# Landmark heads, token stage and passage joined anew in a convolution block, Nystrom attention and expert kernel on Trainium2

## The reference, cut to what matters

```python
# layer 0, per sample: softmax attention with 32 features, then a residual
theta, phi, g = xf @ W_theta + b_theta, xf @ W_phi + b_phi, xf @ W_g + b_g
x = x + softmax(theta @ phi.T) @ g @ W_out + b_out
# layer 1, per sample and head (8 heads of 32): attention through 128 landmarks
q, k, v = heads(layernorm(t) @ w_qkv.T); q *= 32 ** -0.5
q_l, k_l = mean of q and of k over runs of 8 tokens          # 128 landmarks
kernel_1 = softmax(q @ k_l.T); kernel_2 = softmax(q_l @ k_l.T); kernel_3 = softmax(q_l @ k.T)
t = t + (kernel_1 @ (iterative_pinv(kernel_2, 6) @ (kernel_3 @ v))) @ w_out.T + b_out
# layer 2, all tokens: 2 of 16 experts each, gelu between two matrices
t = t + sum of gate_e * (gelu(layernorm(t) @ W1_e) @ W2_e) over a token's two experts
```

## Time and profile before

| what | value |
|---|---|
| median of 3 runs | 1031.95 us (1031.53 to 1034.44) |
| profiled execution | 1034.55 us |
| its span in the trace | 1032.8 us |
| mean granted PE clock | 0.941 of full |
| PE, DVE, ACT, POOL busy | 91%, 55%, 44%, 29% |

### The profile page before, as it was taken

The page is one execution under the profiler, slowest core; times in us unless marked ns, Lnnn a source line. Parts: engine busy times, 40 slices in busy tenths (PEclk is TensorE's granted clock), DMA queues, the critical chain, the costliest instruction groups (busy, mean ns, idle before and its releaser), DMA issues.

```text
span 1032.8 us, 21740 instructions
## 1 busy us (share of the span) xinstructions
PE 936.0 (91%) x6981; PEld 703.6 (68%) x6982; DVE 569.9 (55%) x1585; ACT 449.6 (44%) x1004; POOL 298.1 (29%) x343
## 2 busy tenths in 40 slices
PE   5999989899999899998998998834889999999997
PEld 3565766465776555676655676523779999999996
DVE  3577846486866677775777684676222222222221
ACT  1424376343349352337462337524434444444442
POOL 3150002050000133000122000201357766766664
PEclk9699999698999989999999899955999999999999
DMA  3100000300000120000110000099734444443341
GB/s 102 42 2 1 1 2 25 99 1 1 2 1 2 43 81 1 1 1 2 42 42 1 1 2 1 32 224 314 219 57 71 72 65 67 70 67 63 62 64 18
DMA packets 47847, 50.76 MB, mean 49 GB/s; under 512 B 11072, under 2 KB 41152, under 8 KB 47776
## 3 DMA queue, kind: packets, MB, share of 16 engines
q0 software_dynamic: 15168, 18.85, 11.4%
q1 hardware_dynamic: 32608, 30.99, 9.9%
HBM read 33.00 MB, written 18.78 MB: 50 GB/s over the span
## 4 chain that ended last, share of the span: by engine, by line
PE 76%; DVE 10%; issue 5%; ACT 3%; DMA 3%; POOL 1%; SPq 1%; POOLq 0%; DVEq 0%; ACTq 0%
PE PS L526 13%; PE PS L941 12%; PE PS L950 12%; PE PS L795 7%; PE PS L555 6%; PE PS L587 4%; PE PS L690 3%; PE PS L671 3%; PE PS L598 3%; PE PS L592 3%; DVE neg_max L1161 2%; PE PS L650 2%; DMA low<-rows_scratch,token_of 2%; PE PS L676 2%; PE PS L685 1%
## 5 line engine op out<-in xcount | busy, mean ns | idle before, releaser
L526 PE MATMUL PS<-ident,arena 128*128 128x128 f32 x1016 | 151.1, 298 | 32.6 <-ACT arena L1007 13.3
L526 PEld LDWEIGHTS PS<-ident,arena 128*128 128x128 f32 x1016 | 126.3, 155 | 69.9 <-issue 56.4
L387 POOL TENSOR_SCALAR aggr<-aggr 128x1 f32<-128x1 f32 x64 | 14.2, 222 | 552.9 <-DVE aggr L1264 552.9
L1161 DVE TENSOR_REDUCE neg_max<-PS 128x1 f32<-128x1024 f32 (+1 forms) x96 | 117.5, 1224 | 95.3 <-PE PS L587 41.4
L941 PEld LDWEIGHTS PS<-low 128*128 128x128 f32 x1264 | 154.8, 194 | 4.6 <-DVE low L1570 0.7
L941 PE MATMUL PS<-low 128*128 128x128 f32 x1264 | 155.7, 277 | 0.0
L950 PE MATMUL PS<-arena,low 128*128 x632 | 150.2, 381 | 4.4 <-ACT low L1104 2.9
L435 POOL DMA_INDIRECT out_dram<-low,row_of x79 | 125.4, 1587 | 89.6 <-DVE low L1587 37.6
L1020 ACT COPY arena<-PS 128x1024 f32<-128x1024 f32 x96 | 98.3, 1024 | 96.9 <-PE PS L526 96.7
L950 PEld LDWEIGHTS PS<-arena,low 128*128 128x128 f32 x632 | 113.9, 190 | 18.8 <-issue 6.5
L1104 ACT ACTIVATE low<-PS 128x512 f32<-128x512 f32 x79 | 47.2, 597 | 157.9 <-PE PS L941 128.0
(11 more groups left out here) (202 smaller groups left out, 1323.0 us busy)
## 6 DMA issues: line engine op xcount, KB each, us to landing
arena<-in_L_ffn_W_dram SPq DMA_DIRECT2D x32, 512.0 KB
arena<-in_x_dram SPq DMA_DIRECT2D x4, 1024.0 KB, 6.3
out_dram<-t SPq DMA_DIRECT2D x4, 1024.0 KB, 7.2
rows_scratch<-arena SPq DMA_DIRECT2D x4, 512.0 KB, 3.4
rows_scratch<-arena SPq DMA_DIRECT2D x8, 256.0 KB, 2.6
low<-rows_scratch,token_of POOLq DMA_INDIRECT x79
out_dram<-low,row_of POOLq DMA_INDIRECT x79
arena<-in_L_attn_w_qkv_dram SPq DMA_DIRECT2D x1, 768.0 KB, 4.8
```

Source lines behind the costliest of these rows:

```text
L526: mm = pe.transpose(PS[0:s.shape[1], dst_bank, n * P:n * P + s.shape[0]], s, ident[0:s.shape[0], 0:s.shape[0]])
L1161: dve.tensor_reduce(dst, src, AX.X, ALU.max, negate=True).then_inc(s_max, 1)
```

## The change

The work is the same, and its order in the queues of PE, DVE and ACT changes at the three joins and in the token loop.

- First head: `scores(8)`, `maxima(8)` and `exponentials(8)` go ahead of the matrix pieces on their engines, and `queries(0)` goes ahead of the two transpose pieces.
- Token stage: `scores(16)` no longer waits for `queries(2)`, and `scores(17)` follows `values(14)`, before the last two pieces, which now both use bank 1; `scores(17)` waits for the 29th piece instead of the 32nd. The last piece follows `values(15)`. `queries(2)` comes just before `head_values` (now in bank 0), `queries(3)` after `scores(18)`.
- Token loop: `turn_inverses(s)` stands before `finish` and no longer waits for `out_t`; instead `out_t` waits for the next tile's `turn_inverses`, and `inverses_turned` moves behind `out_t` on DVE.
- Passage: `turn(18)` moves behind `project_tpg(1)` and into banks 2 and 3; `scores(0)`, `scores(1)`, `turn_g` follow. `turn(22)`, `gate` and the transposes back move into the next sample's opening loop (steps s = 0, 1, 2) with their DVE and ACT parts, in banks 1 and 0 (`turn_high` waits for the last normalised rows and for the next sample's g, then does `turn(22)`). On DVE `out_t(23)` goes ahead of the rows of tile 5, and `phi_out`, the last rows and `maxima(0)` are interleaved. After the last sample the router part runs as before.

```diff
+        PIECE_BANK.update({n_pieces - 1: 1, n_pieces: 1})
-                     16: 4, 17: 5, 18: 6, 19: 7, 20: 4, 21: 5, 22: 4, 23: 5}
+        UNIT_BANK.update({18: 2, 19: 3, 22: 1, 23: 0})
+        TURNS = [16, 17, 20, 21, 18, 19, 22, 23]
...
                 if k == 0 and u == 2 * NT + 1:
-                    pe.wait_ge(pinv_ev, (i + 1) * n_pieces)
+                    pe.wait_ge(pinv_ev, (i + 1) * n_pieces - 3)
...
                     if t == 0:
                         pe.wait_ge(pr_used, i * UNITS + 2 * NT)
-                    else:
-                        pe.wait_ge(ot_ready, i * UNITS + 2 * NT + t)
...
+                if i >= 1:
+                    phi_in(i)
+                    for k in range(2):
+                        scores(0, k)
                 for k in range(2):
                     scores(1, k)
-                pe.wait_ge(g_ready, i + 1)
+                if i >= 1:
+                    turn_g(i)
+                    bulk_done(19, i - 1)
                 for s in range(NT + 2):
...
+                    if s == 0 and i >= 1:
+                        turn_high(i - 1)
+                    if s == 1:
+                        pe.wait_ge(g_ready, i + 1)
+                        if i >= 1:
+                            bulk_done(23, i - 1)
+                    if s == 2 and i >= 1:
+                        gate_turned(i - 1)
                     if 1 <= s <= NT:
                         values(s - 1)
+                    if s == 1 and i >= 1:
+                        gate(i - 1)
+                    if s == 2 and i >= 1:
+                        pe.wait_ge(sample_done, i)
                     if s >= 2:
                         finish(s - 2)
...
                 pe.wait_ge(lm_ready, i + 1)
+                for k in range(2):
+                    scores(NT, k)
...
-                for k in range(2):
-                    scores(NT, k)
...
                     if s == NT - 1:
-                        pe.wait_ge(pinv_ev, (i + 1) * n_pieces - 2)
-                        queries(2)
                         pe.wait_ge(q_ready, i * 4 + 2)
...
+                    if s == NT - 1:
+                        for k in range(2):
+                            scores(2 * NT + 1, k)
+                    if s == NT:
+                        inverse_piece(*pieces[-1])
+                    if s == 0:
+                        queries(0)
-                    for piece in mine[0:2]:
+                    for piece in mine[0:2] if s < NT - 1 else mine[0:1]:
                         inverse_piece(*piece)
-                    if s < 2:
-                        queries(s)
+                    if s == 1:
+                        queries(1)
...
                 finish(2 * NT - 1)
-                for k in range(2):
-                    scores(2 * NT + 1, k)
-                pe.wait_ge(q_ready, i * 4 + 4)
+                queries(2)
                 head_values(range(HEADS)).then_inc(y_head_mm, 1)
...
+                    if s < NT:
+                        turn_inverses(s)
                     if s >= 2:
                         finish(2 * NT + s - 2)
-                    if s < NT:
-                        turn_inverses(s)
...
@@ DVE, out_t of a token tile @@
                         dve.wait_ge(inv_copied, i * NT + u - 2 * NT + 1)
+                        if u + 1 < UNITS:
+                            dve.wait_ge(inv_mm, i * NT + u - 2 * NT + 2)
...
@@ DVE, opening loop of the next sample @@
+                    if s == 0 and i >= 1:
+                        bulk(22, xT[:, 0, 512:1024], j=i - 1)
+                    if s == 2 and i >= 1:
+                        logits_out(i - 1)
                     if 1 <= s <= NT:
                         out_t(s - 1)
+                    if s == 1 and i >= 1:
+                        gate_out(i - 1)
...
@@ DVE, token loop @@
+                    if s == NT:
+                        if more:
+                            bulk(20, x0T[:, 0, 512:1024])
+                        out_t(2 * NT + s - 1)
                     if s >= 3:
                         rows1(s - 3)
...
@@ DVE, after the token loop @@
+                if more:
+                    phi_out(i + 1, 0)
+                rows1(NT - 1)
+                if more:
+                    phi_out(i + 1, 1)
+                norm1(NT - 2)
+                if more:
+                    bulk(18, xT[:, 0, 0:512])
+                    maxima(0, i + 1)
                 norm1(NT - 1)
```

More of the change, by code:

```diff
@@ L863, in _ @@
                         turn(16, xs, 0)
-                    if s == NT - 1:
-                        pe.wait_ge(xn2_ready, i * NT + NT // 2)
-                        turn(18, xn, 0)
-                        if more:
-                            turn(20, xs, 1)
+                    if s == NT - 1 and more:
+                        turn(20, xs, 1)
                     if s == NT and more:
@@ L873, in _ @@
                         project_tpg(1)
-                def gate():
-                    for c in range(KC):
-                        for j in range(QUADS):
-                            mm = pe.matmul(PS[HD * j:HD * j + HD, 3, 0:D], wgate_sb[:, c, :], xT[:, c, j * D:(j + 1) * D],
-                                           start=c == 0, stop=c == KC - 1, tile_position=(0, HD * j))
-                    mm.then_inc(gate_mm, 1)
-                pe.wait_ge(xn2_ready, (i + 1) * NT)
-                turn(22, xn, 1)
-                if more:
-                    turn_g(i + 1)
-                bulk_done(23)
-                gate()
-                if more:
-                    phi_in(i + 1)
-                    for k in range(2):
-                        scores(0, k)
-                pe.wait_ge(gate_ready, i + 1)
-                apart(pe, "pe")
-                transposes(pe, 1, [gateT[:, b * P:(b + 1) * P] for b in range(2)]).then_inc(gate_mm, 1)
+                        turn_low(i)
+                    if s == NT and not more:
+                        turn_low(i)
+            turn_high(B - 1)
+            gate(B - 1)
+            gate_turned(B - 1)
             pe.wait_ge(routed, (B + 1) * ROUTE)
@@ L1402, in _ @@
                         out_t(NT + s - 1)
+                    if s == NT - 1:
+                        maxima(2 * NT + 1)
+                        mine = mine[0:1]
+                    if s == NT:
+                        inverse_piece(*pieces[-1])
                     for piece in mine:
@@ L1419, in _ @@
                         counted(i)
-                maxima(2 * NT + 1)
-                for s in range(NT + 3):
-                    if 1 <= s <= NT:
-                        inverses_turned(s - 1)
+                more = i + 1 < B
+                for s in range(NT + 2):
                     if 1 <= s < NT:
```

129 lines of the change are left out of this document (80 added, 49 removed).

## The result

| | before | changed |
|---|---|---|
| median | 1032.69 us (1031.53 to 1034.44, 4 runs) | 1001.87 us (998.46 to 1004.54, 4 runs) |
| profiled execution, its span | 1034.55, 1032.8 us | 999.48, 997.3 us |
| mean granted PE clock | 0.941 | 0.956 |

The ratio is 0.9708, with a 95% interval of 0.9665 to 0.9752: the change makes the kernel about 31 us faster. Forecast were 1008 us, within 999 to 1024. The profiled pair differs by 35.07 us where the sum had 26.6. Executions more than 1.5% above the fastest of the same kernel enter no ratio in what follows; only the token loop alone has such, two of its four.

What follows compares the result with a forecast made beforehand. PE was taken as the bound, busy 91% of the span, with idle gaps and low-clock stretches to win: 12.1 us idle plus 9.3 and 5.2 of clock make 26.6, from 1034.55 to 1008 us, range 999 to 1024.

Steps and rivals of the forecast that it cites:

- 12.1 us of idle time: PE idle time gained over the whole kernel: 5.2 first heads, 3.2 token stage, 1.8 token loop, 1.9 passages.
- 14.5 of clock: Low-clock time won back: all 9.3 us at the first landmark heads and 5.2, half of 10.5, in the passages.
- first head: Gap of 2.41 before turn_probs(8) goes, a new one of 1.1 comes at the norm piece: 1.3 us a sample, 5.2 in all.
- token stage: Where token tiles begin, gaps of 1.4, 0.6 and 0.6 sum to 2.6 against 3.39: 0.8 us a sample, 3.2 in all.
- token loop: turn_inverses loses its wait for out_t, 0.11 us a tile in four tiles of each sample: 1.8 us in all, bounds 0 to 1.8.
- passage: Between samples, gaps of 0.9, 1.05 and 0.9 sum to 2.9 against 3.54: 0.6 us a passage, 1.9 in all.
- the rival in which the clock stays up everywhere: No low-clock stretches at heads or passages: 1034.55 - 12.1 - 19.8 = 1003 us; chance 0.20.
- the router part at its end: End of the last sample: turn(18) moves behind finish(22), but PE's wait there ends as before: 0, within 1 us either way.

Runs made afterwards that it cites:

- the token loop alone: Kernel before with only the token loop's edits (turn_inverses ahead of finish, its wait given to out_t, inverses_turned behind out_t): 998.42, 1000.48, 1015.18 and 1026.42 us.
- the run with the order put back: Changed kernel with finish again ahead of turn_inverses on PE in the token loop, waits as changed: median 1011.13 us, ratio 0.9828 to before.
- the filled kernels: Unread matmuls put in PE waits: kernel before 1009.08 us (0.9814), changed kernel 990.23 (0.963), all edits with ScalarE's bulk(19) copy later 977.97 (0.9508).

## Why the prediction was right, and where it was not

The sum was 12.1 us of idle time and 14.5 of clock. The spans of the profiled pair differ by 35.5 (1032.8 - 997.3). Of these the clock gave 9.6 at the first heads (33.96, 34.11 and 34.12 in samples 1 to 3, less 30.86 each) and 10.5 - 6.4 = 4.1 in the passages, 13.7 in all. The rest, 21.8, is what has to answer to 12.1.

| step | forecast a sample | measured a sample | by |
|---|---|---|---|
| first head | 1.3 | 1.26 | 156.58 - 155.32 |
| token stage | 0.8 | -0.13 | what is left of 156.58 - 152.37 |
| token loop | 0.45 | 3.08 | 156.58 - 153.50 |
| passage | 0.6 | 0.96 | 152.37 - 151.41 |
| sum | 3.15 | 5.17 | 156.58 - 151.41 |

The median of 1001.87 lies inside the range, and nearest to the 1003 of the rival in which the clock stays up everywhere; but the clock did not stay up. In its place stands the token loop, 12.3 us over four samples where I had 1.8, less the token stage, which gave nothing of its 3.2. That two such errors left the time inside the range is in part luck.

- **First head: right in mechanism and size.** The gap of 2.41 went, one of 1.06 (forecast 1.1) came before the norm piece, and the window of 29.6 came out as written.
- **Token loop: the term that was mis-sized.** I priced the removed wait at the idle time shown, 0.11 a tile, and the reordering at nothing. A tile gained 0.47. The order of matmul shapes was worth 0.29 of it, by the run with the order put back. Of the 3.08 a sample, four such tiles make 1.9 and the gap of 1.18 that became 0.73 makes 0.45; the rest lies in the tiles at the loop's ends. The bounds I gave, 0 to 1.8 us in all, did not hold the 12.3 us measured. The trace of before already had a sign of it, which I passed over. In PE's timeline ahead of the passage, `finish` (L690) takes 169.65 - 168.59 = 1.06 where the strips of `turn_inverses` follow, and 177.77 - 176.80 = 0.97 where a full-width product follows:

```profile
168.59 1.13 PE L690 MATMUL PS<-low 128*128 128x256 f32 x4
169.65 0.64 PE L650 MATMUL PS<-ident,head_inv 128*32 128x128 f32 x16
...
176.80 1.13 PE L690 MATMUL PS<-low 128*128 128x256 f32 x4
177.77 1.89 PE L555 MATMUL PS<-arena,low 128*128 128x512 f32 x4
```

- **Token stage: gaps of 1.4, 0.6 and 0.6 were forecast and came as 1.46, 0.64 and 0.81,** but what they gained over the old ones was the loop's. With the loop's edit the old third gap is 0.73, not 1.18, and 1.40 + 0.81 + 0.73 = 2.94 against 2.91 leaves nothing. I had compared with a sum from which another edit of the same change would take a part.
- **Passage: three gaps forecast at 0.9, 1.05 and 0.9, measured 0.97, 1.79 and 0.77.** The chain behind `scores(0)` was right (2.66 forecast; 182.65 less 179.93, the start of `scores(0)` plus 1.06, is 2.72). What differed is that `turn_g` ran within the scores and no longer filled 0.6 of it. So the number came near for another reason than mine. The idle time did not shrink by 0.6: at full clock it is 151.41 - 143.05 = 8.36 a period with the new passage and 152.37 - 144.17 = 8.20 with the old. What shrank is PE's busy time, by 1.12, and the 0.68 of `turn_g` is most of that.
- **The clock: right in size, wrong in how firmly it was put.** The heads gave 9.6 where I had 9.3 (a fall there costs 3.25 in samples 2 and 3, and I took the 3.10 of sample 1 for all), the passages 4.1 where I had 5.2. I reasoned from the trace that a gap of 2.41 brings the clock down three times of four. The loop-only kernel has all these gaps, and its trace shows no fall at any of them. So such a gap is not enough for a fall; that idle time is needed for one is what the filled kernels show. The rule that I had quoted from the Trainium skill ("TensorE: Matmul & The Clock Gate", section "What's actually happening"), that the point of change varies from run to run, fits the three falls of four with the one kernel and none of four with the other. What decides in the single case stays open.
- Three periods of 5.17 make 15.5. The last sample, from its `keys(5)` to its `turn(22)`, gave 3.7 without the clock, where head, stage and loop had 4.2: the router part at its end, forecast at 0 within 1, cost 0.5. The other 2.6 of the 21.8 lie where nothing was changed: 0.4 ahead of the first `keys(5)`, and 2.2 behind the last `turn(22)` (361.9 us to the end of the span before, 359.7 after). The clock has a part in the latter: it falls at the routing in both, but before the transposes of `turn(22)` are done in the one (1.80 us) and behind them in the other (1.09).

## What to carry to other kernels

Filling a wait with matmuls that nobody reads prices the low clock directly: here seven waits of 17 us in all (4 x 2.41 and 3 x 2.45), and one more ahead of the routing, carried 20 us of slower work behind them, which filling them brought out. Take several runs and more than one trace for it: one kernel's trace without a fall says little. When a step moves on TensorE, look at the shapes on either side of its old and its new place, not only at the waits. And when two edits touch one chain of gaps, sum the second against the chain as the first leaves it.

## What the runs showed of the hardware

- Two groups of sixteen matmuls into 32-column strips, one behind the other instead of apart between full-width matmuls, took 0.29 us a tile less (4.01 against 4.30, same waits).
- Transposes of 32 x 32 in partitions 64 to 95 ran within score matmuls of partitions 0 to 63: `scores(0)`, `scores(1)` and `turn_g` took 1.99 us together (178.87 to 180.86), where `scores` take 1.06 each and `turn_g` took 0.68 behind other work.
- The same idle gaps brought the clock down in one trace and not in another: five of seven places in the kernel before, none of seven with the token loop alone. A gap of 1.79 us did so in 14 of 15 passages, one of 1.87 behind full-width transposes in none of three.
- TensorE took up the transposes behind a fill 0.20 us after the exponential that they wait for had ended (78.77 + 1.11 = 79.88, start 80.08), and 0.36 us after it when it had been idle (79.92 + 1.11 = 81.03, start 81.39).
